# Axial attention of a one-core kernel: both axes projected token by token, grams masked as they are rounded, denominators inverted after a turn, new engine orders and PSUM banks

## The reference, cut to what matters

```python
x = x + _L0_conv_ref(_gn(x), Wq, Wk, Wv, bv, Wo, bo, logit_scale, cpb_w1, cpb_b1, cpb_w2)
x = x + _L1_conv_ref(_gn(x), w_qkv0, w_out0, w_qkv1, w_out1)

# the first layer, per window of 64 tokens and head of 16 channels
logits = einsum('bhnd,bhmd->bhnm', qn, kn) * scale + 16.0 * sigmoid(bias)   # masked with -inf
o = einsum('bhnm,bhmd->bhnd', softmax(logits), v)

# the second, per sequence of 16 tokens and head of 16 channels, for each axis
dots = einsum('bhie,bhje->bhij', q, k) * d ** (-0.5)
out = einsum('bhij,bhje->bhie', dots, v)
```

## Time and profile before

| what | value |
|---|---|
| median of 3 runs | 994.42 us |
| profiled execution, span from the first to the last instruction | 996.0 us |
| PE busy | 890.8 us (89%) |
| PE weight loads (PEld) busy | 748.2 us (75%) |
| DVE busy | 828.9 us (83%) |
| ACT busy | 606.4 us (61%) |
| POOL busy | 452.3 us (45%) |
| mean granted TensorE clock | 0.962 of full speed |
| DMA | 385340 packets, 56.98 MB |

### The profile page before, as it was taken

The page is one execution under the profiler, slowest core; times in us unless marked ns, Lnnn a source line. Parts: engine busy times, 40 slices in busy tenths (PEclk is TensorE's granted clock), DMA queues, the critical chain, the costliest instruction groups (busy, mean ns, idle before and its releaser), DMA issues.

```text
span 996.0 us, 41506 instructions
## 1 busy us (share of the span) xinstructions
PE 890.8 (89%) x17568; PEld 748.2 (75%) x17568; DVE 828.9 (83%) x1461; ACT 606.4 (61%) x978; POOL 452.3 (45%) x329
## 2 busy tenths in 40 slices
PE   2267999999999999999999999999999999999965
PEld 2255778888888887888888788788888787878754
DVE  4667989899899998998899899899899897988741
ACT  2334666666676666676676567676666566656631
POOL 5024445445455554544544454444544544444430
PEclk8567999999999999999999999999999999999997
DMA  5100433334344444344344443434344443343443
GB/s 164 36 1 12 55 51 50 50 52 63 61 60 58 60 63 60 56 65 54 59 62 55 59 64 54 63 54 59 61 62 55 59 61 57 57 56 46 57 59 57
DMA packets 385340, 56.98 MB, mean 57 GB/s; under 512 B 349940, under 2 KB 384646, under 8 KB 385158
## 3 DMA queue, kind: packets, MB, share of 16 engines
q1 hardware_dynamic: 385158, 54.33, 36.9%
HBM read 12.30 MB, written 8.40 MB: 21 GB/s over the span
## 4 chain that ended last, share of the span: by engine, by line
PE 79%; ACT 5%; issue 5%; DVE 5%; SPq 3%; POOL 1%; DMA 1%; POOLq 0%; ACTq 0%; DVEq 0%
PE ps L458 26%; PE ps L697 8%; PE ps L605 7%; PE ps L680 6%; PE ps L660 5%; PE ps L650 4%; PE ps L494 4%; PE ps L534 4%; PE ps L681 3%; PE ps L521 3%; PE ps L551 3%; PE ps L745 3%; ACT probs L870 2%; PE ps L727 1%; PE ps L713 1%
## 5 line engine op out<-in xcount | busy, mean ns | idle before, releaser
L1011 POOL TENSOR_TENSOR kv<-kv,kv 128x1024 f16<-128x1024 f32 x64 | 143.8, 2247 | 89.4 <-ACT kv L835 75.8
L1011 POOL TENSOR_TENSOR xn<-xn,xn 128x512 f16<-128x512 f32 x64 | 74.6, 1166 | 174.8 <-ACT xn L865 174.8
L458 PE MATMUL ps<-xn,w_q 128*128 128x256 f16 x1152 | 143.9, 275 | 7.1 <-issue 4.4
L458 PEld LDWEIGHTS ps<-xn,w_q 128*128 128x128 f16 x1152 | 110.9, 101 | 23.1 <-issue 8.0
L846 ACT ACTIVATE gram<-ps 128x1024 f16<-128x1024 f32 x64 | 85.7, 1339 | 56.9 <-PE ps L660 50.8
L680 PE MATMUL ps<-q,gram_wide 128*128 128x32 f16 x2048 | 111.1, 176 | 3.2 <-DMA gram_wide<-gram 2.3
L680 PEld LDWEIGHTS ps<-q,gram_wide 128*128 128x128 f16 x2048 | 110.0, 98 | 3.9 <-DMA gram_wide<-gram 2.4
L1276 DVE RECIPROCAL den_inv<-ps 128x512 f32<-128x512 f32 x32 | 106.8, 3338 | 5.7 <-PE ps L534 5.5
L681 PE MATMUL ps<-q,gram_wide 128*128 128x16 f16 x2048 | 110.6, 169 | 0.0
L1209 DVE SCALAR_TENSOR_TENSOR gram<-ps,gram 128x1024 f16<-128x1024 f32 x64 | 84.4, 1318 | 27.3 <-ACT gram L846 27.3
L681 PEld LDWEIGHTS ps<-q,gram_wide 128*128 128x128 f16 x2048 | 106.0, 97 | 0.3
(11 more groups left out here) (119 smaller groups left out, 1985.9 us busy)
## 6 DMA issues: line engine op xcount, KB each, us to landing
gram_wide<-gram SPq DMA_DIRECT2D x512, 32.0 KB
k_wide<-kv SPq DMA_DIRECT2D x128, 64.0 KB, 2.3
v_wide<-kv SPq DMA_DIRECT2D x256, 32.0 KB, 2.0
x_in<-x SPq DMA_DIRECT2D x32, 128.0 KB
x_in<-x SPq DMA_DIRECT2D x64, 64.0 KB
out<-y_out SPq DMA_DIRECT2D x32, 128.0 KB, 2.4
out<-y_out SPq DMA_DIRECT2D x64, 64.0 KB, 2.1
probs<-L_conv_w_qkv SPq DMA_DIRECT2D x1, 768.0 KB, 5.1
```

The lines of the kernel that those rows point to most:

```text
L458: last = pe.matmul(dst, w[:, wp, c, m * P:m * P + P], act[:, xp, c * TOK:(c + 1) * TOK], start=(n == 0), stop=(n == 5))
L1011: return pool.tensor_tensor(dst, whole, high, ALU.subtract)
```

## The change

**Axis 0 becomes token-major.** `columns_high` (ACT) and `columns_low` (POOL) write a second copy of the normalised activations with the tokens in column order (`xn_cols`, made from the same `xn32`). `axial_kv(0)` then has the form of axis 1 (12 products of 512 columns), and so have `token_copy(0)`, `token_high(0)`, `token_low(0)`, the eight DMAs of `spread_v_rows(0)` and `gram_matmuls(0)`. `turn`, `widen_v`, `kv_high`, `kv_low`, `spread_k` and the tile `k_wide` are gone. q of axis 0 is projected from `xn_cols`, and is rounded without a reordering.

**Grams.** They are rounded in two halves, each multiplied by a mask per partition (`gram_mask`, with the scale in it), so that rows of the other head become zero. Four DMAs of 32 rows per axis then spread them instead of eight of 16.

**Denominators.** TensorE writes each sum once. VectorE turns [128, 256] out of PSUM, takes the reciprocal of 128 x 32, and turns it back repeated 16 times into [128, 512].

**Means.** `group_means` is one product of 12 columns instead of two of 6, and VectorE adds the halves where it copied before.

**Orders and banks.** All five `step(k)` are written in another order, the table of banks is new, and TensorE waits for fewer semaphores. The window part runs one step earlier: `window_qk` of image k is in step k, and TensorE has six stages of steps instead of seven.

```diff
-        QK_BANK, NORM_BANK, V_BANK, DEN_BANK, PV_BANK, Z_BANK = 3, 0, 4, 5, 0, 1
-        S_BANK, KV_BANK, Q_BANK = (3, 6), (3, 6), (3, 2)
-        G_BANK, O_BANK, GM_BANK = (0, 0), (6, 6), (5, 3)
-        Y_BANK, YT_BANK, XT_BANK = 2, 0, 2
+        QK_BANK, V_BANK, DEN_BANK, PV_BANK, Z_BANK, Y_BANK, YT_BANK, XT_BANK = 4, 7, 4, 3, 3, 3, 2, 2
+        S_BANK, KV_BANK, Q_BANK = (5, 3), (5, 6), (5, 2)
+        G_BANK, O_BANK, GM_BANK = (0, 0), (0, 3), (7, 2)
...
             def spread_gram(a, img):
                 reach(sp, gram_lo[a], img)
-                for h in range(8):
-                    rows = slice(DH * h, DH * h + DH)
...
                 for q in range(4):
                     rows = slice(32 * q, 32 * q + 32)
...
             def step(k):
-                for img in there(k - 4):
-                    spread_v_rows(img)
-                for img in there(k - 8):
+                for img in there(k - 5):
+                    spread_v_rows(1, img)
+                for img in there(k - 9):
                     store_image(img)
-                for img in there(k - 4):
-                    spread_gram(0, img)
                 for img in there(k):
                     load_image(img)
+                for img in there(k - 5):
+                    spread_gram(0, img)
+                    spread_gram(1, img)
                 for img in there(k - 4):
-                    spread_gram(1, img)
-                for img in there(k - 3):
-                    spread_k(img)
...
             def window_den(img):
+                reach(pe, probs_ready[1], img)
                 for g in range(G):
-                for pair in range(PAIRS):
-                    g, q = divmod(pair, 4)
-                    last = pe.matmul(ps[32 * q:32 * q + 32, DEN_BANK, g * TOK:(g + 1) * TOK], ones_pair,
-                                     probs[:, place(pair), :], start=True, stop=True)
+                    for q in range(4):
+                        last = pe.matmul(ps[32 * q:32 * q + 32, DEN_BANK, 0:TOK], ones_of[g],
+                                         probs[:, place(4 * g + q), :], start=(g == 0), stop=(g == 1))
...
             def gram_matmuls(a, img):
+                reach(pe, v_spread[a], img, 128)
                 if a == 0:
+                    reach(pe, o1_summed[0], earlier(img, 1))
                 else:
+                    reach(pe, gram_lo[0], img)
...
             def group_means(layer, img):
                 if layer == 0:
+                    reach(pe, v_ready, earlier(img, 1))
+                    edge(pe, gn_small[0], img, GN_STEPS, 4)
                 else:
+                    reach(pe, xt_copied, earlier(img, -2))
+                    reach(pe, gn_small[1], img, GN_STEPS, 4)
-                for h in range(2):
-                    last = pe.matmul(ps[:, GM_BANK[layer], 0:6].rearrange("p (g v) -> p g v", v=3), group8[:],
-                                     halves[:, :, h, :], start=(h == 0), stop=(h == 1))
+                pe.matmul(ps[:, GM_BANK[layer], 0:12], group8[:], stat[layer][:, 0:12],
+                          start=True, stop=True).then_inc(gn_sum[layer], 1)
...
+            def columns_high(img):
+                reach(act, gn_small[1], img, GN_STEPS)
+                reach(act, kv1_proj[0], previous(img))
+                reach(act, q1_proj[0], previous(img))
+                act.activation(in_columns(xn1[0][:, 0, :]), along(xn32[1][:], 0), ACT.Copy).then_inc(xc_hi, 1)
...
+            def columns_low(img):
+                reach(pool, xc_hi, img)
+                low(in_columns(xn1[0][:, 1, :]), along(xn32[1][:], 0), in_columns(xn1[0][:, 0, :])).then_inc(xc_lo, 1)
...
+            def turn_den(img):
+                reach(dve, den_done, img)
+                reach(dve, den_flipped, previous(img))
+                dve.transpose(den_rows[:], ps[:, DEN_BANK, 0:TOK]).then_inc(den_turned, 1)
+
+            def flip_den(img):
+                reach(dve, den_turned, img)
+                reach(dve, den_inverted, previous(img))
+                sums = den_rows[:].rearrange("p (b r) -> p b r", r=32)[:, :, 0:2 * G].rearrange("p b (g h) -> p g b h", g=G)
+                dve.reciprocal(den_cols[:].rearrange("p (g b h) -> p g b h", g=G, h=2), sums).then_inc(den_flipped, 1)
...
-                dve.reciprocal(den_inv[:], ps[:, DEN_BANK, :]).then_inc(den_inverted, 1)
+                dve.transpose(den_inv[:].rearrange("p (x e) -> p x e", e=DH),
+                              den_cols[:].unsqueeze(2).to_broadcast([P, G * BLOCKS * 2, DH])).then_inc(den_inverted, 1)
```

More of the change, by code:

```diff
@@ L749, in step @@
+                pe.matmul(ps[:, GM_BANK[layer], 0:12], group8[:], stat[layer][:, 0:12],
+                          start=True, stop=True).then_inc(gn_sum[layer], 1)
             def step(k):
[L750 to L753, removed]
                 for img in there(k - 2):
-                    window_den(img)
-                    window_pv(img)
-                for img in there(k - 1):
-                    window_qk(img)
+                    window_out(img)
@@ L771, in step @@
                 for img in there(k - 3):
                     axial_q(0, img)
+                for img in there(k - 4):
+                    axial_out(1, img)
+                for img in there(k - 3):
+                    gram_matmuls(0, img)
                 for img in there(k - 1):
                     window_v(img)
+                    scores(img)
                 for img in there(k - 3):
-                    gram_matmuls(0, img)
-                for img in there(k - 2):
-                    group_means(1, img)
@@ L779, in step @@
-                for img in there(k - 4):
-                    axial_out(1, img)
+                    axial_q(1, img)
                 for img in there(k):
@@ L783, in step @@
                 for img in there(k - 3):
-                    axial_q(1, img)
+                    gram_matmuls(1, img)
+                for img in there(k - 2):
+                    axial_kv(0, img)
                 for img in there(k - 1):
-                    scores(img)
-            over_steps(step, 7)
+                    window_den(img)
+                for img in there(k - 5):
+                    result_rows(img)
+                for img in there(k - 1):
+                    window_pv(img)
+                for img in there(k):
+                    window_qk(img)
+                for img in there(k - 3):
+                    axial_out(0, img)
+            over_steps(step, 6)
         @block.scalar
@@ L1048, in step @@
             def step(k):
-                for img in there(k - 3):
-                    token_low(img)
                 for img in there(k - 1):
@@ L1061, in step @@
                     normed_low(0, img)
+                for img in there(k - 2):
+                    normed_low(1, img)
+                for img in there(k - 1):
+                    o_low(img)
+                for img in there(k - 2):
+                    token_low(0, img)
                 for img in there(k - 4):
```

489 lines of the change are left out of this document (183 added, 306 removed).

## The result

The change makes the kernel slower: 1006.92 us in the median of 4 runs (1001.51 to 1008.73) against 994.62 (4 runs, 994.28 to 995.65). The ratio is 1.012, with a 95% interval of 1.0095 to 1.0145. The forecast was 969 us, in a range of 947 to 990, with a chance of 0.10 for slower.

A forecast was written before the change was run, and what follows sets the result against it. TensorE was taken as the bound: 26.41 work + 0.5 waits + 0.4 holes = 27.3 us a step against 28.05, saving 21.7 over 29 steps. With 3.5 from filling and draining, span 996.0 becomes 970.8, time 969 us; range 947 to 990.

The forecast's parts named there:

- the waits of the new order: TensorE's waits for results in the rewritten step: together 0.4 to 0.7 us a step, taken as 0.5.
- TensorE's work: TensorE's products in one step: 26.88 us falls by 0.47 to 26.41, mostly from halved group_means.
- DVE's relief: VectorE's work per step: net 4.3 us less of some 26, with DVE busy near 700 us.
- Scores to sums: TensorE's wait of 0.54 us for the exponentials: goes, with 5.6 us of cover for a need of 4.6.
- v to the means: group_means(0) waiting for spread_v, behind gram_high(0) and columns_high on ScalarE: a wait of about 0.35 us.
- `columns_low`: Rival, strided copy on GpSimd: at three times 1.17 us, PE waits 0.7 more a step, about 989 us; chance 0.04.
- The v rows of axis 1: k-v projection to grams of axis 1: wait 0 to 0.3 us; as slower rival, 1007 or 1021 us, chance 0.10.
- The holes: "Issue" gaps in TensorE's axis 1 grams: 0.4 us a step for 0.63; rival stay or grow, 989 us, chance 0.09.
- Filling and draining: Before the third image and after the last window_den: filling +1 us, draining 66 for 70.3, so -4.5.
- The last term of the sum: From profiled span to median time: the median is 1.6 us below the span, so 970.8 becomes 969.
- 0.88 for faster: Chance of a gain over 0.2%: 0.62 own case, 0.13 all in time, 0.09 holes, 0.04 slow copy.
- the single rivals: All in time (949 us, 0.13), holes stay or grow (0.09), v rows bound (0.10), slow copy on POOL (0.04).

The follow-up runs named there:

- e1: The changed kernel with the small statistics group_moments(0) moved behind o1_sum(0) and q1_low(0) on VectorE: 989.28 us, 0.9943 of the kernel before.
- e6: e5 with only four of the eight DMAs for the v rows of axis 1, so half are left out of the grams: 965.62 us, ratio 0.9713.
- e8: e5 with the v half of axis 1's tokens copied, rounded and subtracted first, its DMAs waiting for that alone; nothing left out: 968.65 us, ratio 0.9719.
- e7: The kernel before with only the denominators turned (reciprocal of 128 x 32 in place of 128 x 512): 994.11 us, ratio 0.9997.
- e5: e1 with spread_v put ahead of columns_high on ScalarE: 986.89 us, 0.992 of the kernel before.
- e9: The changed kernel with only four of eight DMAs for the v rows of axis 1, half left out of the grams: 998.09 us, ratio 1.0024.
- e10: The changed kernel in its own order, with layer 0's squared means in PSUM instead of SBUF: 988.28 us, 0.9923 of the kernel before.
- e4: The kernel before with only the means changed to one product of 12 columns per group norm: 991.61 us, ratio 0.9983.

## Why the prediction was wrong

**The step that failed** is "the waits of the new order", 0.5 us a step: VectorE's operations were laid out at their bare length, wherever they fell. I checked each chain for the results it waits for, and not what runs on GpSimd beside it. `group_moments(0)` fell under `qk_low`, and its 0.17 us became 2.07. Two things followed. The wait of the grams of axis 0 for `o1_sum(0)`, which is in no item of the forecast's list and so was put at nothing, is 0.96 us: TensorE was there 10.2 us into the step, as laid out, and `o1_sum(0)` ended at 11.0. And `group_norm(1)`, laid out to end at 13.4, ended at 14.3 (528.71, with the step's start at 514.45), which delays `columns_high` and `spread_v`. Instead of 26.9 us (0.5 of waits on 26.41 of work) the calm step has 28.18. Moving the statistics gives back 0.98 of that (27.20 in e1). The trace of before held the hint (0.32 for 0.16 us), and I did not read instructions of 0.3 us.

**TensorE's work**: right. e6 and e8 run at 26.95 with 0.4 us a step of waits for `columns_low`, which leaves 26.5 to 26.6 for the 26.41 predicted.

**DVE's relief**: nearly right, once the standstill is taken out. DVE is busy 759 us, not "near 700", and 55 of that is the standstill (L1044 holds 65.8 where e1 has 10.6), which leaves 704. The single terms were a little low: the new operations take 0.45 + 0.35 + 0.71 = 1.51 us for the 1.23 I had, and the halves of `gram_low` cost more than two starts (1.48 us for 1.32). Free time on VectorE was worth nothing by itself (e7).

```profile
L1153 DVE STREAM_TRANSPOSE den_rows<-ps 128x256 f32<-128x256 f32 x32 | 14.4, 450 | 13.1 <-PE ps L498 12.8
L1160 DVE RECIPROCAL den_cols<-den_rows 128x32 f32<-128x32 f32 x32 | 11.3, 353 | 1.1
L1165 DVE STREAM_TRANSPOSE den_inv<-den_cols 128x512 f32<-128x512 f32 x32 | 22.8, 711 | 1.1
L752 ACT ACTIVATE xn_cols<-xn 128x512 f16<-128x512 f32 x32 | 34.7, 1086 | 9.0 <-DVE xn L1070 8.3
L900 POOL TENSOR_TENSOR xn_cols<-xn,xn_cols 128x512 f16<-128x512 f32 x32 | 45.3, 1415 | 90.5 <-ACT xn_cols L752 90.5
```

**The single chains.** Scores to sums: right, that wait is gone. v to the means: right in place, 0.68 us in e1's calm steps for 0.35, since `columns_high` takes 1.09 us and not the 0.6 of a packed copy. `columns_low` takes 1.42 for 1.17, a fifth more; by the Trainium skill's rule that the forecast quoted (GPSIMD Engine Reference, "Performance pitfalls for Q7 kernels") it would have been half more, and the measurement decides (of the two inputs only one is read with the step). The v rows of axis 1: right that they are just in time, but too cheap at 0 to 0.3. GpSimd ends `token_low(1)` at 522.70 (520.56 + 2.14), and the eight DMAs behind it are issued by 528.69, in 6.0 us where eight took 5.06 (the row below holds both spreads, with a pause between them): one issue of the eight took 1.5 us and the others 0.6. Why is open. In e5 the chain from the k-v projection to the grams is so 12.9 us for a cover of 11.6, and the wait 1.30. The standstill hid this in the changed kernel. Without the standstill and with the v rows late, e5 is at 987 us: inside the forecast's range, and 18 us above its 969.

Queue of SP, and POOL's `token_low(1)`, in the changed kernel:

```profile
515.12 13.57 SPq L400 DMA_DIRECT2D v_wide<-kv  x16
```

```profile
520.56 2.14 POOL L900 TENSOR_TENSOR kv<-kv,kv 128x1024 f16<-128x1024 f32 x1 [4.35 <-ACT kv L709]
```

**The holes**: they vanished from the changed kernel's steady steps, better than the 0.4 I took. With them gone and TensorE waiting on others, nearly every step is alike. No run moved the dense products alone, so that their new place is what did it is not shown.

**Filling and draining.** Filling was nearly right (111.84 for 113.1). Draining was 66 by my layout and is 77.3: TensorE waits twice over 3 us for v rows there and once 4.60 us for gram rows. Behind these waits `axial_y` takes 4.49 us where it took 2.78 in the middle: the granted clock is 0.61 of full in that stretch, which mixes the two levels, where it was 1.00 from 970 to 978. e9 says that 6 us of the draining are the v rows'. The last term of the sum, 1.6 us from the span down to the time, had the wrong sign: the one execution of the changed kernel with both numbers has a span of 1006.9 us and a time of 1008.73.

Timeline of PE, then the stretches (us, busy us of PE, PEld, DVE, ACT, POOL, granted clock, DMA share, GB/s):

```profile
952.46 2.75 PE L570 MATMUL ps<-v_wide,kv 128*32 128x256 f16 x48 [3.17 <-DMA v_wide<-kv]
...
978.10 1.49 PE L570 MATMUL ps<-v_wide,kv 128*32 128x256 f16 x48 [3.25 <-DMA v_wide<-kv]
...
984.78 0.21 PE L584 MATMUL ps<-q,gram_wide 128*128 128x32 f16 x1 [4.60 <-DMA gram_wide<-gram]
...
986.51 4.49 PE L596 MATMUL ps<-o,w_o 128*128 128x256 f16 x24
```

```profile
970.00:978.00 8.00, 4.86 (x128) 4.16 (x126) 3.89 (x6) 3.71 (x6) 1.84 (x2) 1.00 0.18 47
986.50:991.00 4.50, 4.50 (x30) 3.11 (x27) 0.00 (x0) 0.60 (x1) 0.00 (x0) 0.61 0.55 144
```

**The chances.** 0.88 for faster rested on one schedule in which five waits lay within 0.5 us of their cover. I had counted this for the single rivals and not for what I could not see: a schedule as tight as that passes on a delay from an engine that none of the five names.

## What to carry to other kernels

When an order is rewritten by hand or by a planner, ask of each VectorE instruction with two SBUF inputs what GpSimd runs at that moment: it may cost the rest of that operation, however small it is. One masking with a single SBUF input was held too, so read the trace for the others. Put such an instruction where GpSimd is idle, or give it one operand in PSUM. Then look at the tiny instructions of the trace first: a mean of 1029 ns on 128 x 4 numbers, beside neighbours at 165, found 18 us. And when one delay is taken away, expect the next one under it: here the standstill (18 us) and the v rows (18 us more, from e5 to e8) lay in the same shadow.

## What was new on the hardware

A VectorE instruction with two SBUF inputs is held to the end of GpSimd's subtraction (2.07, 1.77, 1.55 and 1.18 us in four kernels, each to within 0.1 us of GpSimd's end), and one with a PSUM input at the same moment is not (0.16 us in e10). A masking with one float16 input in SBUF was held once in the kernel before (2.35 us for 0.48). The holes in TensorE's stream ("issue", up to 1.8 us at the grams of axis 1, about every third step before, up to 2.2 us in e4) are gone in the changed kernel's order; what sets their length, and which part of the change removes them, stays open.
